# A sparse graph layer on one core: the matrix read in 8 KB runs, x and out moved four tiles at a time

## What is computed

```python
h = max(layernorm(x), 0)
mask = adj > 0
head = mask / max(sqrt(sum(mask * mask, axis=-1)), 1e-12)
inc = adj + head
x = x + (inc @ h) / sum(inc, axis=-1)
```

## Time and profile before

| | |
|---|---|
| median of 3 runs | 1267.18 us (1265.48 to 1268.1) |
| the profiled execution | 1265.03 us |
| its span (first to last instruction) | 1263.2 us |
| DVE busy | 1162.8 us (92%) |
| ACT busy | 977.8 us (77%) |
| PE busy | 970.4 us (77%) |
| POOL busy | 764.9 us (61%) |
| moved by DMA | 471.29 MB, mean 373 GB/s |

### The profile page before, as it was taken

The page is one execution under the profiler, slowest core; times in us unless marked ns, Lnnn a source line. Parts: engine busy times, 40 slices in busy tenths (PEclk is TensorE's granted clock), DMA queues, the critical chain, the costliest instruction groups (busy, mean ns, idle before and its releaser), DMA issues.

```text
span 1263.2 us, 14630 instructions
## 1 busy us (share of the span) xinstructions
PE 970.4 (77%) x2678; PEld 482.8 (38%) x2678; DVE 1162.8 (92%) x2794; ACT 977.8 (77%) x1903; POOL 764.9 (61%) x745
## 2 busy tenths in 40 slices
PE   0002889988888888888888888798888878878676
PEld 0001334444444434444433444344444434434343
DVE  6679999999999999999998999989999989998972
ACT  6657888898888887888887787788878778876551
POOL 1003666766666667676666666775666667667453
PEclk9999999888889999889988988988899889998698
DMA  9999999999999999999999999999999999999442
GB/s 360 428 421 406 398 402 392 392 394 399 396 391 402 401 399 398 384 401 394 384 398 368 400 398 391 388 395 373 402 400 400 385 382 387 398 399 355 142 143 79
DMA packets 148127, 471.29 MB, mean 373 GB/s; under 512 B 24386, under 2 KB 24386, under 8 KB 143876
## 3 DMA queue, kind: packets, MB, share of 16 engines
q1 hardware_dynamic: 90368, 331.38, 66.9%
q0 software_dynamic: 57664, 138.93, 29.9%
HBM read 490.21 MB, written 33.82 MB: 415 GB/s over the span
## 4 chain that ended last, share of the span: by engine, by line
DVE 45%; DMA 20%; issue 20%; ACT 5%; SPq 5%; another core or an unknown queue 2%; PE 1%; DVEq 0%; ACTq 0%; POOL 0%; POOLq 0%
DMA adj_tile<-in_adj_dram 17%; DVE folded L774 15%; DVE cand_word L779 12%; DVE cand_index L783 5%; DMA gathered_rows<-in_x_dram 3%; SPq L385 2%; ACT junk L569 2%; DVE cand_word L797 2%; SPq L392 2%; DVE cand_index L802 2%; ACT adj_tile L556 2%; SPq L396 1%; DVE ln_stats L757 1%; DVE weights_and_payload L914 1%
## 5 line engine op out<-in xcount | busy, mean ns | idle before, releaser
L488 POOL DMA_INDIRECT gathered_rows<-h_scratch,slot_column x520 | 536.8, 1032 | 265.9 <-issue 161.2
L569 ACT ACTIVATE junk<-adj_tile,zero_unit 128x2048 bf16<-128x2048 f32 x256 | 510.1, 1994 | 111.2 <-issue 75.5
L1330 PE MATMUL acc<-gathered_rows,diag 128*128 128x512 f32 x1040 | 504.1, 641 | 0.5 <-issue 0.5
L488 POOL DMA_INDIRECT gathered_rows<-h_scratch,spill_column x197 | 220.5, 1119 | 199.0 <-ACT spill_column L615 150.8
L774 DVE SCALAR_TENSOR_TENSOR folded<-adj_tile 128x1024 f32<-128x1024 f32 x248 | 301.4, 1215 | 12.1 <-DMA adj_tile<-in_adj_dram 10.7
L1330 PEld LDWEIGHTS acc<-gathered_rows,diag 128*128 128x128 f32 x1040 | 213.7, 212 | 247.1 <-issue 246.8
L779 DVE MAX8 cand_word<-folded 128x8 f32<-128x1024 f32 x248 | 302.9, 1221 | 2.2
L783 DVE FIND_INDEX8 cand_index<-cand_word,folded 128x8 uint32<-128x1024 f32 x248 | 302.2, 1218 | 0.0
L1341 PE MATMUL acc<-gathered_rows,spill_matrix 128*128 128x512 f32 x394 | 186.3, 607 | 14.6 <-issue 10.7
L632 ACT ACTIVATE diag<-ident,weights_and_payload 128x128 f32<-128x128 f32 x582 | 176.2, 387 | 0.5 <-DVE weights_and_payload L914 0.5
L1278 PE MATMUL poff<-spill_rank,lanes_before 128*128 128x1 f32 x130 | 26.4, 272 | 187.5 <-DVE spill_rank L859 174.4
(11 more groups left out here) (146 smaller groups left out, 829.8 us busy)
## 6 DMA issues: line engine op xcount, KB each, us to landing
adj_tile<-in_adj_dram SPq DMA_DIRECT2D x256, 1024.0 KB
h_scratch<-adj_tile SPq DMA_DIRECT2D x16, 1024.0 KB, 10.5
out_dram<-out_tile SPq DMA_DIRECT2D x64, 256.0 KB
gathered_rows<-in_x_dram SPq DMA_DIRECT2D x12, 1024.0 KB, 12.6
x_residual<-in_x_dram SPq DMA_DIRECT2D x48, 256.0 KB
gathered_rows<-h_scratch,slot_column POOLq DMA_INDIRECT x520
x_held<-in_x_dram SPq DMA_DIRECT2D x4, 1024.0 KB, 7.9
gathered_rows<-h_scratch,spill_column POOLq DMA_INDIRECT x197
```

Source lines behind the costliest of these rows:

```text
L488: nc.gpsimd.indirect_dma_start(out=into, out_offset=None, in_=h[:, :], in_offset=bass.IndirectOffsetOnAxis(ap=column, axis=0), bounds_chec ...
L569: nc.scalar.activation(junk[:, n % 2].rearrange("p (j c) -> p j c", j=2), both[:, :, half], ACT.Relu, bias=zero_unit[:], scale=-UP, accum_ ...
L1330: last = nc.tensor.matmul(acc[t % 3][:], diag[:, t % 2, 1 + s], slot(t % 2, s), start=False, stop=False)
```

## The change

The chunk j of a tile is now the columns 2048j to 2048j + 2047, 8 KB in a row for each partition, and the fold lays its second 1024 columns over its first 1024. The four groups of places are those four blocks, and the constants that turn places into columns follow. x and out go in blocks of four tiles: a block is 128 runs of 8 KB, 1 MB. `held` has room for five blocks instead of four, in a ring; ACT writes the output of a tile over its x, SP stores a whole block, and loads block c of x into the place of block c - 5 once that is stored. `xres` and `osb` are gone, and with them the waits on `res_added` (SP) and on `out_stored` (ACT). The batch tile takes four spill groups instead of three, and one step of DVE's last tests goes.

```diff
-    HELD_CHUNKS = 4
+    HELD_CHUNKS = 5
...
-    x_t = x.rearrange("(c p j) d -> c j p d", p=P, j=ROWS)
-    out_t = out.rearrange("(c p j) d -> c j p d", p=P, j=ROWS)
-    adj_h = adj.rearrange("(c p j) (h n) -> c j p h n", p=P, j=ROWS, h=2)
+    out_ln = out.rearrange("(c p j) d -> c p j d", p=P, j=ROWS)
+    adj_t = adj.rearrange("(c p j) n -> c j p n", p=P, j=ROWS)
...
-        held = sb("x_held", [P, HELD, D], fp32)
-        xres = sb("x_residual", [P, 2, D], fp32)
+        held = sb("x_then_out", [P, HELD, D], fp32)
...
-        osb = sb("out_tile", [P, 2, D], fp32)
...
         def x_of(t):
-            return held[:, t] if t < HELD else xres[:, t % 2]
+            return held[:, t % HELD]
+        def group(c):
+            k = c % HELD_CHUNKS
+            return held[:, ROWS * k:ROWS * (k + 1), :]
+        def out_of(t):
+            return again[:] if t == BATCH else held[:, t % HELD]
+        def x_come(t):
+            c = t // ROWS
+            return x_loaded[c % 2], 16 * ((c - HELD_CHUNKS) // 2 + 1)
...
         def groups(t):
-            return EXTRA if FOLDED <= t < BATCH else FOLDED_EXTRA
+            return EXTRA if wide(t) else FOLDED_EXTRA
...
-                sp.dma_start(chunk(t % 2, j), adj_h[t // ROWS, t % ROWS, :, :, CW * j:CW * (j + 1)]).then_inc(adj_loaded[t % 2][j], 16)
-            def load_x(t):
-                if t >= HELD + 2:
-                    sp.wait_ge(res_added, t - 1)
-                    if not wide(t - 2):
-                        sp.wait_ge(row_ready, t - 1)
-                sp.dma_start(xres[:, t % 2], x_t[t // ROWS, t % ROWS]).then_inc(x_loaded[t % 2], 16)
-            def store_tile(t):
-                sp.wait_ge(out_ready, t + 1)
-                sp.dma_start(out_t[t // ROWS, t % ROWS], osb[:, t % 2]).then_inc(out_stored[t % 2], 16)
+                sp.dma_start(A[:, t % 2, 2 * CW * j:2 * CW * (j + 1)],
+                             adj_t[t // ROWS, t % ROWS, :, 2 * CW * j:2 * CW * (j + 1)]).then_inc(adj_loaded[t % 2][j], 16)
+            def load_x(c):
+                sp.wait_ge(out_stored[(c - HELD_CHUNKS) % 2], 16 * ((c - HELD_CHUNKS) // 2 + 1))
+                sp.dma_start(group(c), x_ln[c]).then_inc(x_loaded[c % 2], 16)
+            def store_group(c):
+                sp.wait_ge(out_ready, ROWS * c + ROWS)
+                sp.dma_start(out_ln[c], group(c)).then_inc(out_stored[c % 2], 16)
...
-                if t >= 4:
-                    store_tile(t - 4)
-                if t >= HELD:
-                    load_x(t)
+                if t >= 2 * ROWS and t % ROWS == 0:
+                    store_group(t // ROWS - 2)
+                if t % ROWS == 2 and HELD_CHUNKS <= t // ROWS - 2 + HELD_CHUNKS < LN:
+                    load_x(t // ROWS - 2 + HELD_CHUNKS)
...
-            for t in range(TILES - 4, TILES):
-                store_tile(t)
+            for c in range(LN - 2, LN):
+                store_group(c)
...
-            count_up(base_own[:, 0], [[0, 2], [CW, CHUNKS]], int(SKIP), 0)
+            count_up(base_own[:, 0], [[0, 2], [2 * CW, CHUNKS]], int(SKIP), 0)
...
             def finish_tile(t):
                 act.wait_ge(acc_ready, t + 1)
-                if t >= 2:
-                    act.wait_ge(out_stored[t % 2], 16 * (t // 2))
-                nc.scalar.activation(osb[:, t % 2], acc[t % 3][:], ACT.Copy).then_inc(out_ready, 1)
+                nc.scalar.activation(out_of(t), acc[t % 3][:], ACT.Copy).then_inc(out_ready, 1)
...
-                nc.vector.scalar_tensor_tensor(out=ranked(cola[:], t), in0=ranked(ge[:], t), scalar=float(HALF),
+                nc.vector.scalar_tensor_tensor(out=ranked(cola[:], t), in0=ranked(ge[:], t), scalar=float(CW),
...
-                step(nc.vector.scalar_tensor_tensor(out=w_well[:, 6, TILES - FOLDED:], in0=end_all[:, BATCH:BATCH + 1],
-                                                    scalar=float(FOLDED_EXTRA * P),
-                                                    in1=w_well[:, 5, TILES - FOLDED:], op0=ALU.is_le, op1=ALU.add))
```

More of the change, by code:

```diff
@@ L206, in diag_chunk @@
         def diag_chunk(t):
-            return t // ROWS * P * ROWS % HALF // CW
+            return t // ROWS * P * ROWS // (2 * CW)
         def diag_column(t):
-            k = t // (TILES // 2) * 8 + t % 8
-            return diag_at[:, k:k + 1]
+            return diag_at[:, t % 16:t % 16 + 1]
         def cands(t):
@@ L242, in searched @@
             return CHUNKS * min(t, FOLDED) + PARTS * max(t - FOLDED, 0)
-        def part(i):
-            return i % 2 * CHUNKS + i // 2
         def paid(t, k):
@@ L314, in add_graph_layer @@
         spill_gathered = [sem(f"spill_gathered{b}") for b in range(2)]
-        res_added = sem("res_added")
         row_added = sem("row_added")
@@ L434, in _ @@
                     sp.dma_start(A[:, 0, :], adj[bass.ds(row, P, step=ROWS), :]).then_inc(d_adj, 16)
-                    sp.dma_start(xres[:, 0], x[bass.ds(row, P, step=ROWS), :]).then_inc(d_x, 16)
+                    sp.dma_start(held[:, 0], x[bass.ds(row, P, step=ROWS), :]).then_inc(d_x, 16)
                     for c in range(NCH):
@@ L440, in _ @@
                     sp.wait_ge(d_out, j + 1)
-                    sp.dma_start(out[bass.ds(row, P, step=ROWS), :], osb[:, 0]).then_inc(d_stored, 16)
+                    sp.dma_start(out[bass.ds(row, P, step=ROWS), :], held[:, 1]).then_inc(d_stored, 16)
                     sp.wait_ge(d_stored, j * 16 + 16)
@@ L536, in _ @@
             for b in range(2):
-                pool.wait_ge(out_stored[b], 16 * (TILES // 2))
+                pool.wait_ge(out_stored[b], 16 * (LN // 2))
             pool.wait_ge(out_ready, BATCH + 1)
@@ L639, in row_again @@
                 if t >= HELD:
-                    act.wait_ge(x_loaded[t % 2], 16 * x_turn(t))
+                    act.wait_ge(*x_come(t))
                 c, j = t // ROWS, t % ROWS
@@ L786, in part_columns @@
             def part_columns(t, i):
-                if t == BATCH:
-                    return A[:, 0, CW * part(i):CW * (part(i) + 1)]
-                return chunk(t % 2, part(i) % CHUNKS)[:, part(i) // CHUNKS]
+                return A[:, t % 2, CW * i:CW * (i + 1)]
             def part_values(t, i):
@@ L794, in part_values @@
                 else:
-                    dve.wait_ge(adj_loaded[t % 2][part(i) % CHUNKS], 16 * turn(t))
-                e = slice(8 * part(i), 8 * part(i) + 8)
+                    dve.wait_ge(adj_loaded[t % 2][i // 2], 16 * turn(t))
+                e = slice(8 * i, 8 * i + 8)
                 nc.vector.max(out=cv[:, t % 2, e], in_=part_columns(t, i)).then_inc(vals_found, 1)
@@ L1265, in _ @@
                     dve.wait_ge(d_x, j * 16 + 16)
-                    nc.vector.scalar_tensor_tensor(out=osb[:, 0], in0=pdense[:], scalar=drd[:], in1=xres[:, 0],
+                    nc.vector.scalar_tensor_tensor(out=held[:, 1], in0=pdense[:], scalar=drd[:], in1=held[:, 0],
                                                    op0=ALU.mult, op1=ALU.add).then_inc(d_out, 1)
@@ L1316, in residual @@
                 elif t >= HELD:
-                    pe.wait_ge(x_loaded[t % 2], 16 * x_turn(t))
-                nc.tensor.matmul(acc[t % 3][:], ident[:], again[:] if t == BATCH else x_of(t), start=True,
-                                 stop=False).then_inc(res_added, 1)
+                    pe.wait_ge(*x_come(t))
+                nc.tensor.matmul(acc[t % 3][:], ident[:], again[:] if t == BATCH else x_of(t), start=True, stop=False)
                 if not wide(t):
```

10 lines of the change are left out of this document (4 added, 6 removed).

## The result

| | before | after |
|---|---|---|
| median of 6 runs each | 1266.6 us | 1275.48 us (1269.01 to 1280.06) |
| ratio, 95% interval | | 1.007 (1.004 to 1.010) |
| the profiled execution | 1265.03 us | 1269.01 us |
| its span | 1263.2 us | 1267.3 us |
| mean granted clock of TensorE | 0.908 | 0.937 |

The account below looks back on a forecast made before the run. DVE's pace was taken to bound the kernel up to 347 us, then DMA's supply. Profiled 1265.0 - 21 (DMA time) - 0.4 (start) + 1.4 (end) = 1245.0; the median, 2.2 us higher, gave 1247 us, range 1239 to 1264.

Parts of the forecast that it names:

- The DMA time saved where DMA sets the pace is 21 us: Main stage from about tile 16: fewer packets 18.4, fewer DMAs 0.2, x held longer 2.5 us of DMA time.
- I take 21: Main stage: all 21 us saved reach the run time, between bounds of 11 and 26 us.
- the 26 us of idle time: DVE from 347 to 1126 us: idle time that a faster supply can give back at most.
- At that level PE's work doesn't fit the pace, PE falls behind, and 3 x 5 us reach DVE: Main stage: PE at 1.2 GHz, its lower clock, was held to cause DVE's three waits at L941, 13.0 us together.
- gathers starve: Rival, main stage: longer packets delay the gathers' queue, PE's lead is used up, slower at 1282 us; chance 0.13.
- PE keeps its delays: Rival, main stage: DMA's own waits go, three 5 us waits tied to PE's clock stay, 1256 us; chance 0.22.
- 8 KB is no cheaper in the mix: Rival, main stage: beside gathers longer adj packets save nothing, only x and out gain, 1262 us; chance 0.15.
- The order on SP and the bursts, cost 0: SP's queue: later waits and 1 MB bursts before adj chunks cost nothing; bound +67 us, given no weight.
- Before the first full tile, -0.4: Before 98 us: five adj chunks in 8 KB runs save 0.4 us.
- The 0.2 us for fewer DMAs: Main stage: 15 fewer DMAs in ten tiles save their small packets, 0.2 us in all.
- The end, +1.4: Batch tile at the end: the fourth spill group adds passes on PE's unbroken chain, 0.85 and 0.55 us.
- its lead of 9.7 us: Main stage: PE's lead over DVE's `find_entry` (L941); once used up, every half-clock time was to reach DVE.

Follow-up runs that it names:

- `no_x_loads`: `after_4k_comb` without the loads of x in the main stage (output differs from tile 20 on): 1228.15 us, 0.979 of the kernel before.
- `before_third`: The kernel before, unchanged, profiled again on a chip of the faster kind: 1253.0 us.
- `after_comb`: Changed kernel, adj still in 8 KB runs, x and out blocks by four DMAs of every fourth partition, one a period: 1250.86 us, 0.9963 of the kernel before.
- `after_batch_three`: Changed kernel with three spill groups for the batch tile instead of four: 1768.69 us, 1.409 of the kernel before.
- `before_again`: The kernel before, unchanged, timed and profiled again on a chip of the slower kind: 1265.15 us.
- experiment 7: Changed kernel and its twin with adj in two 4 KB-run DMAs a chunk, on one slower-kind chip: 1280.39 and 1273.74 us, 1.014 and 1.008 of the kernel before.
- `xo_spread`: Kernel before with x and out in 8 KB runs, each block by four DMAs of 32 neighbouring partitions, one a period: 1332.07 us, 1.052.
- experiments 1 and 2: Halves of the change apart: x and out alone 1.0015, adj alone 1.410, `after_batch_three` 1.409; then the changed kernel with 4 KB adj runs, 1.0017.
- `xo_comb`: Kernel before with x and out in 8 KB runs, each block by four DMAs of every fourth partition, one a period: 1254.37 us, 0.9994.
- `after_adj_4k`: Changed kernel with each adj chunk in two DMAs of 4 KB runs: 1257.09 us, 1.0017 of the kernel before.
- `after_4k_comb`: `after_adj_4k` with x and out blocks by four DMAs of every fourth partition, one a period: 1250.34 us, 0.9954 of the kernel before.
- `after_third`: The changed kernel, unchanged, timed again on a chip of the slower kind: 1280.39 us, 1.014 of the kernel before.
- `after_4k_third`: Changed kernel with each adj chunk in two DMAs of 4 KB runs, on the same slower-kind chip as `after_third`: 1273.74 us, 1.008 of the kernel before.
- `before_two_dmas`: Kernel before with each adj chunk in two DMAs, left and right half, still 4 KB runs: 1250.67 us, 0.9967 of the kernel before.

## Why the prediction was wrong, by its own steps

- **"The DMA time saved where DMA sets the pace is 21 us" and "I take 21": this step failed**, in its second half. The DMA time was saved (13.5 us in 750), and a packet does cost about 9 ns: 65,536 more of them cost 31 us where 37 were worked out before what hides. Saved DMA time also counts where it is taken away (`no_x_loads`). But it was taken by making the packets of adj longer, and that held back the gathers on the other queue: the 26 us of idle time were not given back, they changed their cause. On B, waits for adj fell from 27.5 to 1.1 us and 22.9 us of waits behind PE and for the gathers took their place (`before_third`, `after_comb`); in the first profiles DVE's waits, all causes together, went from 27.3 to 27.2 us. Measured in place of 21 us: the main stage got 1.0 us shorter in the first profile, 3.7 on B (`after_batch_three`), longer in both later profiles on A (last fold at 1150.4 and 1155.3 us, `before_again` 1144.1). The reason given, that DVE had kept its pace for 249 us wherever supply was enough, says nothing of the gathers, for which PE hardly waited in that trace (13.3 us, all causes together).
- **"At that level PE's work doesn't fit the pace, PE falls behind, and 3 x 5 us reach DVE"** is a misreading of the earlier trace rows. PE's products were done 9 to 11 us before DVE came to wait (experiment 7), and on B the same kernel (`before_third`) has no wait at L941 before 1130 us, at a granted clock of 0.90 from 347 to 1126 us and of 0.57 from 647 to 657 us, against 0.91 and 0.57 in the first profile.
- **The rival "gathers starve"** was right in kind. PE's waits for gathered rows are what it said they would be, and they vanish with 4 KB runs. It was given 0.13 and was too large (1282, measured 1275.5): it let half of a clock loss of 70 us through, while the granted clock rose instead, from 0.91 to 0.94 (0.95 in `after_comb`). That isn't simply PE standing still more: in `xo_spread` PE is busy for even less of that stretch (633.57 us) and was granted 0.86. Its argument against, one microsecond in which q0 had 72 packets beside 29, says how packets are shared, not when a gather lands. The Trainium skill ("DMA: Bandwidth & Descriptors", section "Queues, rings and completion order") has an engine go round its queues a packet at a time, where its packet is a bundle of typically 9 to 17 descriptors (orders to move one stretch of bytes), so it is not the packet that the profile counts and that the rival reckoned with. PE's waits for gathered rows on one chip, 143.8 us with 8 KB runs and 4.6 us with 4 KB (experiments 1 and 2), agree with such turns in direction; how they are shared was not measured.
- **The rival "PE keeps its delays"** was right that the three waits at L941 are no DMA waits and that such waits would stay: 13.0 us before, 9.2 us after in the main stage. It was wrong about their cause, as above, and it left out that all waits for what comes from PE would grow: `remote` waits from 97 us on go from 50.7 to 95.1 us in sum.
- **"8 KB is no cheaper in the mix"**: wrong for adj and undecided for x and out. Those had 46 x 0.11 + 2.5 = 7.6 us coming; `xo_comb` gave 0.8 (0.9994, at most 2.5). Its queue q1 was 68.5% busy in 750 us against 69.5 in `before_third`, so 7.5 us of that queue's time were saved there too; q0 has 32.7% against 32.5, and DVE waited for adj about as long as before (25.9 us against 27.5). Why isn't settled.
- **The order on SP and the bursts, cost 0**: about right with adj in one DMA for a chunk, as in the change (blocks instead of four DMAs of every fourth partition cost 0.2%, doubling the bursts added 0.1%), wrong with two: 0.6% between `after_adj_4k` and `after_4k_comb`, on two B chips.
- **Before the first full tile, -0.4**: not seen (the first fold starts at 78.8 us, 78.6 before). The 0.2 us for fewer DMAs would be 69 x 16 x 9 / 16 = 0.6 us by the prediction's own 9 ns for a packet; nothing hangs on it.
- **The end, +1.4**: too small. On B the end after the last fold takes 113.3 to 115.2 us in the four kernels with four groups (`after_adj_4k`, `after_comb`, `after_4k_comb`, `no_x_loads`) and 110.0 to 113.3 in those with three, so about +2.8 by the means, 114.2 and 111.4. In the first profiles on A it was +5.1, but there 22.0 us of `remote` waits at L936 lie in it, against 6.2 at L941 before.
- **Shown or argued.** Shown: 8 KB runs of adj cause the gathers' delay; PE's delay replaces the waits for adj; so on B the saved DMA time buys little. Not shown: that the 8 KB runs by themselves make the kernel slower. The pairs that differ in them differ in the number of DMAs for a chunk too: `after_third` and `after_4k_third` on A (6.7 us, with overlapping intervals), `after_comb` and `after_4k_comb` on two B chips (0.9963 and 0.9954, no difference to be seen). The changed kernel itself was never timed on B. Argued only: that on A the late gathers and the late signals of PE meet and use up its lead of 9.7 us, while on B the lead takes the gathers alone. Why PE's signals come late on A, and what else of the change costs there (the places, the fourth group, the blocks; `after_4k_third` has all three and two DMAs), stays open.
- **The fastest versions**, 0.9954, 0.9963 and 0.9967, can't be told apart. The cheapest edit is `before_two_dmas`. None of them was run on an A chip.

## What to carry to other kernels

Longer packets on one queue save time per packet and are paid for by the small transfers on another: before lengthening a bulk load, find the engine that waits for the gathers beside it and how much lead it has. Saved transfer time is worth its full size only if every engine that shared the wait had something else to spare; from the idle time of the busiest engine that you hope to win, take off what would end it next. Before you build on the cause that a profile gives for a wait, look whether the update that ended it is in the trace, and when. And measure on more than one chip: one and the same version cost 0.8% on one kind of chip and 0.17% on the other.

## What I had not expected of the hardware

- Two kinds of chip: the same kernel takes 1265 or 1255 us. In the main stage both are alike (last fold at 1139.8 and 1144.1, against 1140.7 us); the end takes 123.4 and 119.3 us against 110.6. Only the slower kind has updates of PE's semaphore `brought` that come up to 15.3 us after the product, and its traces hold 8,687 to 11,137 updates in all, those of the other kind 20,534 to 26,051.
- A DMA of 32 neighbouring partitions (8 KB each) slows the whole main stage to 360 GB/s, from 392 with every fourth partition: 5% of the time, for two such DMAs of 256 KB in a period. The first is from an A chip, the second from a B chip; `before_again` on the A chip moves 391 GB/s.
- Each load of 1 MB of adj in two DMAs of 512 KB, the runs and bytes unchanged, made the kernel before 0.33% faster (0.9967, 0.9955 to 0.998).
